# Graph transformer in one launch: the attention's query loads are issued by ScalarE instead of SyncE

## The chip, the cores and the metric

The kernel runs on one core of one Trainium2 chip. The metric is the device time of one execution in microseconds (us). The time before is the median of three runs, 3420.31 us (3411.84 to 3421.84).

## The reference

A graph of 2500 nodes and 40000 edges passes one graph convolution and then a two-layer graph transformer. The attention is over the edges; the kernel computes it densely, with a mask made of edge counts. What matters here is one attention layer:

```python
q = ((x @ Wq[l].T + bq[l]) * scaling).reshape(n, H, DH)      # n = 2500, H = 8, DH = 64
k = (x @ Wk[l].T).reshape(n, H, DH)
v = (x @ Wv[l].T).reshape(n, H, DH)
scores = jnp.einsum('ehd,ehd->eh', q[tgt], k[srcidx])
m = jax.ops.segment_max(scores, tgt, num_segments=n)
p = jnp.exp(scores - m[tgt])
s = jax.ops.segment_sum(p, tgt, num_segments=n)
w = p / (s[tgt] + 1e-16)
agg = jax.ops.segment_sum(w[:, :, None] * v[srcidx], tgt, num_segments=n)
attn = agg.reshape(n, D) @ Wo[l].T + bo[l]
```

## The kernel before

The program has a front (edge counts, graph convolution, first projections), then for each of two layers an attention and a feed-forward part, with projections between the layers, and a final norm. The change is in `attention`, which runs once per layer.

The targets are cut into 20 tiles of 125 nodes, and a tile has 8 heads. A tile and a head make a **unit**, so a layer has 160 units, numbered `u`; `u % 8` is the head, and this text calls the unit with `u % 8 == 0` the tile's unit 0. The 2500 sources are cut into five **chunks** of 500, `k` or `c` from 0 to 4. Each engine has its own program, written out unit by unit and chunk by chunk, and semaphores alone tie them together:

- TensorE scores a chunk against the tile's queries (`score`, L1393), two units ahead of the rest.
- VectorE adds the mask and takes the running maximum (`add_bias`, L1546), then the row's maximum (`maximum`, L1552). At the end of a tile's unit 0 it also scales the sums of the tile before (`normalise`, L1571 to L1578).
- ScalarE takes the exponentials of the next unit in three pieces (`exps`, L1483, which waits for the maximum with `maxed`).
- The weights must be transposed before they multiply the values. Chunks 1 and 3 are transposed by TensorE (`turn_weights`, L1404; then ScalarE's high half L1493 and VectorE's low half L1559). Chunks 0, 2 and 4 are split into two halves in f16 in one of three `staged` buffers (high half by GpSimd for chunks 0 and 2 and by ScalarE for chunk 4, both L1317; low half by GpSimd, L1323), and a DMA transposes the buffer into one of four `across` buffers. That DMA is issued by SyncE (`turn`, L1347). A `staged` buffer is free again when its transposing DMA has landed (`crossed`).
- TensorE multiplies by the values, three chunks later in its own order (`weigh`, L1424).

SyncE issues every transfer of the attention, in one order on one DMA queue: the three transposing DMAs of each unit, one chunk of the next tile's mask before units 1 to 5 (`load_mask`, L1338, two DMAs for 112 and 13 rows), once a layer the output weights (L1364), and the next tile's queries before the transposing DMAs of unit 0 (`load_queries`, L1332, two DMAs of 64 rows with 4000 bytes each, one to each half of the partitions). The queries have two buffers. So their load waits for the maxima of the tile that used the buffer last:

```python
if h == 0:
    if t > 1:
        sp.wait_ge(maxed, U0 + H * (t - 1))
    load_queries(t)
```

Of the kernel before, what the change touches and what calls it, by code (L numbers as in the profile page):

```python
# [30 lines left out]
H = 8  # L31
DH = D // H
# [6 lines left out]
NT = N // P  # L39
# [66 lines left out]
def apart(engine, waits_met):  # L106

    engine.sem_inc(waits_met, 1)
# [1107 lines left out]
def attention(nc, sem, psum, sb, g, layer):  # L1217

    xt, keys, values, vec, q_tiles = g["xt"], g["keys"], g["values"], g["vec"], g["q_tiles"]
    bias_rows, identity, stats = g["bias_rows"], g["identity"], g["stats"]  # L1220
    U0, T0 = UNITS * layer, NT * layer
    EXPS = ((0, 2), (2, 4), (4, 5))
    with ExitStack() as ctx:
        wo_sb = sb(ctx, "wo_sb", [128, FC, D])
        queries = [sb(ctx, f"queries{b}", [128, H, 2, P], F16) for b in range(2)]
# [24 lines left out]
        q_loaded = [sem("q_loaded0"), sem("q_loaded1")]  # L1250
# [3 lines left out]
        maxed = sem("maxed")  # L1254
# [22 lines left out]
        def pe_chunk(u, k):  # L1277
            return len(BY_PE) * (U0 + u) + BY_PE.index(k)

        def dma_chunk(u, k):  # L1280
            return len(BY_DMA) * (U0 + u) + BY_DMA.index(k)

        def dma_chunk_at(n):
            return n // len(BY_DMA), BY_DMA[n % len(BY_DMA)]
# [14 lines left out]
        def use(what, where, part):  # L1299
            n = len(USERS) * layer + USERS.index((what, where, part))  # L1300
            return n, n % TB
# [18 lines left out]
        def low_to_stage(engine, u, k):  # L1320
# [3 lines left out]
                                 prob[u % PROBS][:, k * KC:(k + 1) * KC].rearrange("p (s c) -> p s c", s=BPC),  # L1324
                                 here[0:P, 0:BPC, 0:P], ALU.subtract).then_inc(low_staged[k], 1)

        with nc.Block() as block:
            @block.sync
            def _(sp):
                def load_queries(t):  # L1330
                    for half in range(2):
                        sp.dma_start(queries[t % 2][64 * half:64 * half + 64, :, :, :].rearrange("d h s n -> d (h s n)"),  # L1332
                                     q_tiles[t * DH:(t + 1) * DH, :]).then_inc(q_loaded[t % 2], 16)

                def load_mask(t, c):
                    at = slice(c * KC, (c + 1) * KC)
                    for p0, p1 in CUTS:
                        sp.dma_start(bias[t % 2][p0:p1, at], bias_rows[P * t + p0:P * t + p1, at]).then_inc(mask_loaded[t % 2], 16)  # L1338

                def turn(u, k):  # L1340
                    n = dma_chunk(u, k)
                    if n >= ACROSS:
                        before, chunk = dma_chunk_at(n - ACROSS)
                        sp.wait_ge(weighted, NKC * before + chunk + 1)
                    sp.wait_ge(low_staged[k], U0 + u + 1)
                    apart(sp, g["waits_met"])
                    sp.dma_start_transpose(across[n % ACROSS][:, :, :], staged[n % STAGES][:, :, :].rearrange("p s c -> p (s c)")  # L1347
                                           ).then_inc(crossed[n % ACROSS], 16)

                load_queries(0)  # L1350
                for c in range(NKC):
                    load_mask(0, c)
                for u in range(UNITS):
                    t, h = u // H + 1, u % H
                    if t < NT:

                        if h == 0:
                            if t > 1:
                                sp.wait_ge(maxed, U0 + H * (t - 1))
                            load_queries(t)  # L1360
                        if 0 < h <= NKC:
                            load_mask(t, h - 1)
                        if t == 1 and h == NKC + 1:
                            sp.dma_start(wo_sb[:, :, :].rearrange("p c d -> p (c d)"), g["wo"][layer * 128:(layer + 1) * 128, :]  # L1364
                                         ).then_inc(wo_loaded, 16)
                    for k in BY_DMA:
                        turn(u, k)
# [108 lines left out]
            @block.scalar  # L1476
            def _(act):
                def exps(u, piece):
                    if piece == 0:
                        act.wait_ge(maxed, U0 + u + 1)  # L1480
                    c0, c1 = EXPS[piece]
                    here = prob[u % PROBS][:, c0 * KC:c1 * KC]
                    act.activation(here, here, ACT.Exp, bias=neg_max[u % 4][:, :],  # L1483
                                   accum_out=sums[u // H % 2][:, u % H, piece:piece + 1]).then_inc(exped, 1)

                def high_half(u, k):
                    n, r = use("P", u, k)
                    m = pe_chunk(u, k)
                    act.wait_ge(turned, n + 1)
                    if m >= PB:  # L1490
                        unit, at = divmod(m - PB, len(BY_PE))
                        act.wait_ge(weighted, NKC * unit + BY_PE[at] + 1)
                    act.copy(p_hi[m % PB][:, :], t_ps[r][0:P, 0:KC]).then_inc(p_high, 1)  # L1493

                def read_high(u):
                    act.wait_ge(weighted, NKC * (U0 + u + 1))
                    reached(act, agg_out, U0 + u - 1)
                    act.copy(by_high[u % 2][:, :], o_ps[u % 2][:, 0:DH]).then_inc(high_out, 1)

                def turned_sums(t, half):  # L1500
                    n, r = use("T", t, half)
                    act.wait_ge(turned, n + 1)
                    act.copy(agg_t[t % 2][:, half * 2 * P:(half + 1) * 2 * P], t_ps[r][:, 0:2 * P]).then_inc(agg_turned, 1)  # L1503

                def stage_highs(u, step):

                    for k in BY_DMA:
                        if HIGH_BY[k] == "ACT" and step == min(k // 2 * 2 + 1, NKC - 1):
                            high_to_stage(act, act.copy, u, k)

                for piece in range(len(EXPS)):
                    exps(0, piece)
                for step in range(NKC):
                    stage_highs(0, step)
                for u in range(UNITS):
                    for k in range(NKC):
                        if k in BY_PE:
                            high_half(u, k)
                        if k == LAG and u > 0:
                            read_high(u - 1)  # L1520
                        if k % 2 == 0 and u + 1 < UNITS:
                            exps(u + 1, k // 2)
                        if u + 1 < UNITS:
                            stage_highs(u + 1, k)
                        step = extra_before(u, k)
                        if step and step[0] == "T" and u > H:
                            turned_sums(u // H - 1, step[1])
                read_high(UNITS - 1)
                for half in range(2):
                    turned_sums(NT - 1, half)  # L1530
# [404 lines left out]
```

## Time and profile before

| | |
|---|---|
| median of three runs | 3420.31 us |
| the profiled execution's own time | 3432.88 us |
| its span, first to last instruction | 3431.1 us |
| TensorE's mean granted clock | 0.971 |
| TensorE matmul busy | 3127.8 us (91%) |
| VectorE busy | 2318.9 us (68%) |
| GpSimd busy | 2158.9 us (63%) |
| ScalarE busy | 1954.3 us (57%) |
| DMA queue q1 (SyncE's) | 439.75 MB |
| DMA queue q10 (ScalarE's) | 31.19 MB |

The profile is of one execution, which took 12.57 us longer than the median of the runs; every duration below is from it. The two attention layers are the stretches from about 984 to 1975 us and from 2300 to 3287 us of the span. Times within a view are microseconds from the start of the span, and square brackets in a view hold the time that the engine stood idle ahead of the instruction, and what ended that.

### The profile page before, as it was taken

The numbers are of one execution on the slowest core, as the hardware profiler recorded it, in microseconds if no ns is written. First come the engines' busy times: TensorE is split into PE (matmuls) and PEld (weight loads), VectorE is DVE, ScalarE is ACT, GpSimd is POOL, SyncE is SP. The second block draws the span as 40 slices with busy tenths as digits, with TensorE's granted clock in tenths as the row PEclk, the third lists the DMA queues.
The fourth block names the chain that finished last, engine by engine and source line by source line (L and its number), as shares of the span: only waits on it lengthen the run. The fifth ranks groups of instructions, "written<-read, shape, count | busy, mean of one in ns | idle before, by whom it ended". The sixth has DMA issues, their size and how long they took to land. (4 is left out here: it accounts for less than half of the span.)

```text
span 3431.1 us, 72840 instructions
## 1 busy us (share of the span) xinstructions
PE 3127.8 (91%) x25127; PEld 2478.9 (72%) x25127; DVE 2318.9 (68%) x6932; ACT 1954.3 (57%) x3918; POOL 2158.9 (63%) x1981
## 2 busy tenths in 40 slices
PE   6477999999869999999999989989999999999985
PEld 6343665566548888888888876757888888888874
DVE  7996443443247888888788752237788888888856
ACT  0122444444347777877777711237777777777724
POOL 3788888885047777777777700026777777777734
PEclk9998999999989999999999989999999999999987
DMA  9315667765589999999999811249999999989851
GB/s 341 32 2 104 120 121 124 133 116 113 156 179 167 162 159 169 172 162 164 163 164 163 143 50 37 51 96 170 165 163 164 165 170 167 169 160 169 151 116 60
DMA packets 1290929, 476.32 MB, mean 139 GB/s; under 512 B 1236080, under 2 KB 1261330, under 8 KB 1284873
## 3 DMA queue, kind: packets, MB, share of 16 engines
q1 hardware_dynamic: 1152130, 439.75, 66.9%
q0 software_dynamic: 133120, 0.80, 4.2%
q10 hardware_dynamic: 5320, 31.19, 2.6%
q8 instruction: 199, 3.26, 0.4%
q14 instruction: 160, 1.31, 0.1%
HBM read 133.23 MB, written 80.32 MB: 62 GB/s over the span
## 5 line engine op out<-in xcount | busy, mean ns | idle before, releaser
L1546 DVE CUSTOM_DVE_ANT_0 prob<-s_ps,mask 125x500 f32<-125x500 f32 x1600 | 1058.2, 673 | 307.1 <-PE s_ps L1393 230.5
L1323 POOL TENSOR_TENSOR staged<-prob,staged 125x500 f16<-125x500 f32 x960 | 1067.2, 1117 | 169.1 <-ACT staged L1317 106.6
L1483 ACT ACTIVATE prob<-prob,neg_max 125x1000 f32<-125x1000 f32 (+1 forms) x960 | 954.5, 994 | 123.7 <-DVE scrap L1552 122.6
L1393 PE MATMUL s_ps<-keys,queries 128*125 128x500 f16 x3200 | 946.9, 378 | 39.5 <-DMA queries<-q_tiles 27.0
L529 POOL DMA_INDIRECT counts<-count,cell x320 | 652.8, 2040 | 165.1 <-issue 100.8
L1424 PEld LDWEIGHTS o_ps<-values,across 125*125 125x125 f16 x7680 | 593.3, 139 | 221.8 <-issue 71.1
L1424 PE MATMUL o_ps<-values,across 125*125 125x128 f16 x7680 | 609.4, 223 | 57.2 <-DMA across<-staged 56.2
L1317 POOL CAST staged<-prob 125x500 f16<-125x500 f32 x640 | 385.4, 602 | 390.1 <-ACT prob L1483 248.4
L1559 DVE TENSOR_TENSOR p_lo<-t_ps,p_hi 125x500 f16<-125x500 f32 x640 | 431.9, 675 | 94.9 <-ACT p_hi L1493 94.5
L1404 PE MATMUL t_ps<-identity,prob 125*125 125x125 f32 x2560 | 413.2, 284 | 8.4 <-ACT agg L1503 8.2
L1493 ACT CAST p_hi<-t_ps 125x500 f16<-125x500 f32 x640 | 361.9, 565 | 93.1 <-PE t_ps L1404 92.7
L1393 PEld LDWEIGHTS s_ps<-keys,queries 128*125 128x125 f16 x3200 | 354.9, 139 | 52.7 <-DMA queries<-q_tiles 28.7
L1424 PE MATMUL o_ps<-values,p_hi 125*125 125x128 f16 x2560 | 365.8, 222 | 1.7 <-DVE p_lo L1559 1.7
L1424 PE MATMUL o_ps<-values,p_lo 125*125 125x128 f16 x2560 | 364.6, 222 | 0.0
L1424 PEld LDWEIGHTS o_ps<-values,p_hi 125*125 125x125 f16 x2560 | 323.2, 138 | 52.2 <-DVE p_lo L1559 2.8
L1424 PEld LDWEIGHTS o_ps<-values,p_lo 125*125 125x125 f16 x2560 | 312.2, 139 | 47.3 <-issue 0.6
L1317 ACT CAST staged<-prob 125x500 f16<-125x500 f32 x320 | 195.6, 611 | 259.4 <-issue 204.9
L1404 PEld LDWEIGHTS t_ps<-identity,prob 125*125 125x125 f32 x2560 | 331.7, 189 | 13.2 <-ACT prob L1483 11.0
L1372 POOL MEMSET staged<- 128x1024 f16 x6 | 5.5, 951 | 446.9 <-POOLq L1123 312.1
L1483 ACT ACTIVATION_READ_ACCUMULATOR prob<-prob,neg_max 125x1 f32 x960 | 185.5, 193 | 0.0
L1446 PE MATMUL t_ps<-agg,wo_sb 128*128 128x125 f32 x1280 | 181.1, 287 | 1.1 <-ACT agg L1503 1.1
L969 PE MATMUL agg_ps<-values,turned 125*125 125x512 f32 x400 | 181.2, 592 | 0.0
(170 smaller groups left out, 3900.6 us busy)
## 6 DMA issues: line engine op xcount, KB each, us to landing
mask<-bias_rows SPq DMA_DIRECT2D x200, 218.8 KB
counts<-xt ACTq DMA_DIRECT2D x8, 3054.0 KB, 34.5
keys<-counts SPq DMA_DIRECT2D x40, 546.9 KB
bias_rows<-edge_bias SPq DMA_DIRECT2D x20, 1093.8 KB
queries<-q_tiles SPq DMA_DIRECT2D x80, 250.0 KB, 4.5
across<-staged SPq DMA_TRANSPOSE x960, 3.3
q_tiles<-q_both SPq DMA_DIRECT2D x80, 125.0 KB, 3.0
counts<-count,cell POOLq DMA_INDIRECT x320
```

Of the source, the lines that this page charges most:

```text
L529: pool.indirect_dma_start(counts, bass.IndirectOffsetOnAxis(cell[:, c:c + 1], 0), count[:, c:c + 1], None, compute_op=ALU.add).then_inc(gr ...
L969: mm = pe.matmul(agg_ps[t % 2][0:P, :], lhsT=turned_sb[u % 2][0:P, j * P:(j + 1) * P], rhs=hw(s), start=(s == 0), stop=(s == NT - 1))
L1317: copy(staged[n % STAGES][0:P, 0:BPC, 0:P], prob[u % PROBS][:, k * KC:(k + 1) * KC].rearrange("p (s c) -> p s c", s=BPC)).then_inc(high_st ...
L1323: engine.tensor_tensor(here[0:P, BPC:2 * BPC, 0:P], prob[u % PROBS][:, k * KC:(k + 1) * KC].rearrange("p (s c) -> p s c", s=BPC), here[0:P ...
L1393: mm = pe.matmul(s_ps[n % SB][:, 0:KC], lhsT=queries[b][:, h, part, :], rhs=keys[:, h, c * KC:(c + 1) * KC], start=(part == 0), stop=(part ...
L1404: mm = pe.transpose(t_ps[r][0:P, s * P:(s + 1) * P], prob[u % PROBS][:, (k * BPC + s) * P:(k * BPC + s + 1) * P], identity[0:P, 0:P])
L1424: mm = pe.matmul(o_ps[u % 2][:, 0:2 * DH], lhsT=weights[:, s * step:s * step + P], rhs=values[:, u % H, k * BPC + s, :], start=(k == 0 and ...
L1446: mm = pe.matmul(t_ps[r][:, 0:P], lhsT=wo_sb[:, k, o * 128:(o + 1) * 128], rhs=agg_t[t % 2][:, k * P:(k + 1) * P], start=(k == 0), stop=(k ...
L1483: act.activation(here, here, ACT.Exp, bias=neg_max[u % 4][:, :], accum_out=sums[u // H % 2][:, u % H, piece:piece + 1]).then_inc(exped, 1)
L1493: act.copy(p_hi[m % PB][:, :], t_ps[r][0:P, 0:KC]).then_inc(p_high, 1)
L1546: dve.tensor_tensor_reduce(out=prob[u % PROBS][:, at], in0=s_ps[n % SB][:, 0:KC], in1=bias[b][:, at], scale=1.0, scalar=MASKED, op0=ALU.ad ...
L1559: dve.tensor_tensor(p_lo[m % PB][:, :], t_ps[r][0:P, 0:KC], p_hi[m % PB][:, :], ALU.subtract).then_inc(bank_read, 1)
```

## The change

`load_queries` takes the issuing engine as an argument. ScalarE issues the first tile's queries at the start of the attention, ahead of its first exponential. It issues the queries of tile `t` in unit 0 of tile `t - 1`, right behind the first piece of the next unit's exponentials, and ahead of that it waits for the maxima of the tile before. SyncE keeps its own wait for these maxima, since the mask's buffer needs it too, and keeps the masks, the output weights and all transposing DMAs.

```diff
+        def load_queries(engine, t):
+            for half in range(2):
+                engine.dma_start(queries[t % 2][64 * half:64 * half + 64, :, :, :].rearrange("d h s n -> d (h s n)"),
+                                 q_tiles[t * DH:(t + 1) * DH, :]).then_inc(q_loaded[t % 2], 16)
+
         with nc.Block() as block:
             @block.sync
             def _(sp):
-                def load_queries(t):
-                    for half in range(2):
-                        sp.dma_start(queries[t % 2][64 * half:64 * half + 64, :, :, :].rearrange("d h s n -> d (h s n)"),
-                                     q_tiles[t * DH:(t + 1) * DH, :]).then_inc(q_loaded[t % 2], 16)
-
...
-                load_queries(0)
                 for c in range(NKC):
                     load_mask(0, c)
                 for u in range(UNITS):
                     t, h = u // H + 1, u % H
                     if t < NT:
 
-                        if h == 0:
-                            if t > 1:
-                                sp.wait_ge(maxed, U0 + H * (t - 1))
-                            load_queries(t)
+                        if h == 0 and t > 1:
+                            sp.wait_ge(maxed, U0 + H * (t - 1))
                         if 0 < h <= NKC:
                             load_mask(t, h - 1)
...
+                load_queries(act, 0)
                 for piece in range(len(EXPS)):
                     exps(0, piece)
...
                         if k % 2 == 0 and u + 1 < UNITS:
                             exps(u + 1, k // 2)
+                        if k == 0 and u % H == 0 and u // H + 1 < NT:
+
+                            if u > 0:
+                                act.wait_ge(maxed, U0 + u)
+                            load_queries(act, u // H + 1)
                         if u + 1 < UNITS:
                             stage_highs(u + 1, k)
```

SyncE, around the second tile's unit 0, before the change. `across_0` and `staged_0` stand for all buffers of these names.

```order
452 L1347 DMA_TRANSPOSE across_0<-staged_0 128x8x128 [waits weighted,low_staged4]
453 L1332 DMA queries_0<-q_tiles 64x2000 [waits maxed]
454 L1332 DMA queries_0<-q_tiles 64x2000
455 L1347 DMA_TRANSPOSE across_0<-staged_0 128x8x128 [waits weighted,low_staged0]
456 L1347 DMA_TRANSPOSE across_0<-staged_0 128x8x128 [waits weighted,low_staged2]
457 L1347 DMA_TRANSPOSE across_0<-staged_0 128x8x128 [waits weighted,low_staged4]
458 L1338 DMA mask_0<-bias_rows 112x500
459 L1338 DMA mask_0<-bias_rows 13x500
```

The same place on SyncE with the change.

```order
450 L1347 DMA_TRANSPOSE across_0<-staged_0 128x8x128 [waits weighted,low_staged4]
451 L1347 DMA_TRANSPOSE across_0<-staged_0 128x8x128 [waits low_staged0,maxed,weighted]
452 L1347 DMA_TRANSPOSE across_0<-staged_0 128x8x128 [waits weighted,low_staged2]
453 L1347 DMA_TRANSPOSE across_0<-staged_0 128x8x128 [waits weighted,low_staged4]
454 L1338 DMA mask_0<-bias_rows 112x500
455 L1338 DMA mask_0<-bias_rows 13x500
```

The two query loads ahead of the three transposing DMAs of unit 0 are gone from SyncE, and the wait on `maxed` moved to the first of these three.

ScalarE in the same unit, before the change.

```order
454 L1317 CAST staged_0<-prob_0 125x4x125 [waits stages_cleared,crossed3,exped]
455 L1483 ACTIVATE prob_0,sums_0<-prob_0,neg_max_0 125x1000 [waits maxed]
456 L1493 CAST p_hi_0<-t_ps_0 125x500 [waits weighted,turned]
457 L1483 ACTIVATE prob_0,sums_0<-prob_0,neg_max_0 125x1000
458 L1493 CAST p_hi_0<-t_ps_0 125x500 [waits weighted,turned]
```

ScalarE there with the change (the lines of `attention` behind the moved function are three lower).

```order
456 L1317 CAST staged_0<-prob_0 125x4x125 [waits stages_cleared,crossed3,exped]
457 L1480 ACTIVATE prob_0,sums_0<-prob_0,neg_max_0 125x1000 [waits maxed]
458 L1329 DMA queries_0<-q_tiles 64x2000 [waits maxed]
459 L1329 DMA queries_0<-q_tiles 64x2000
460 L1490 CAST p_hi_0<-t_ps_0 125x500 [waits weighted,turned]
461 L1480 ACTIVATE prob_0,sums_0<-prob_0,neg_max_0 125x1000
462 L1490 CAST p_hi_0<-t_ps_0 125x500 [waits weighted,turned]
```

The two query loads now stand between the next unit's first exponential and the high half of this unit's chunk 1.

## Rows read from the trace of the kernel before

**Rows 1.** Windows view: us, PE, PEld, DVE, ACT, POOL busy, PEclk, DMA share, GB/s

```profile
984.00:1975.00 991.00, 953.68 (x9924) 819.86 (x9925) 799.45 (x2558) 757.62 (x1627) 715.63 (x795) 0.99 0.94 163
```

**Rows 2.** Waits of TensorE in the first layer (total us, times, longest)

```profile
PE o_ps L1424 <- DMA across<-staged: 31.0, 31, 3.7
...
PE s_ps L1393 <- DVE chunk_max L1546: 3.2, 6, 0.6
```

**Rows 3.** Waits of TensorE in the second layer

```profile
PE o_ps L1424 <- DMA across<-staged: 25.3, 29, 3.3
```

**Rows 4.** Timeline of TensorE: chunk 0 of unit 0 in four tiles; chunk 4 in one

```profile
1087.58 0.59 PE L1424 MATMUL o_ps<-values,across 125*125 125x128 f16 x7 [1.51 <-DMA across<-staged]
...
1187.56 0.65 PE L1424 MATMUL o_ps<-values,across 125*125 125x128 f16 x8 [0.89 <-DMA across<-staged]
...
1191.62 0.63 PE L1424 MATMUL o_ps<-values,across 125*125 125x128 f16 x8
...
1928.32 0.63 PE L1424 MATMUL o_ps<-values,across 125*125 125x128 f16 x8
...
3190.70 0.47 PE L1424 MATMUL o_ps<-values,across 125*125 125x128 f16 x5 [0.30 <-DMA across<-staged]
```

**Rows 5.** Timeline of SyncE around unit 0 of the fifth tile

```profile
1180.30 1.23 SPq L1332 DMA_DIRECT2D queries<-q_tiles  x2
1181.65 5.84 SPq L1347 DMA_TRANSPOSE across<-staged  x3
1187.55 1.02 SPq L1338 DMA_DIRECT2D mask<-bias_rows  x2
```

**Rows 6.** Tile view: transposing DMAs issued at 1181.65, 1183.02 and 1924.63

```profile
DMA to landing us min/median/max: 5.8/5.8/5.8
...
DMA to landing us min/median/max: 5.2/5.2/5.2
...
DMA to landing us min/median/max: 3.0/3.0/3.0
```

**Rows 7.** Tile view of all transposing DMAs, then of all query loads

```profile
L1347 SPq DMA_TRANSPOSE across<-staged x960: 1230/1237/4584, 981.0 to 3281.5; - x192
...
DMA to landing us min/median/max: 3.0/3.3/7.5
...
DMA to landing us min/median/max: 3.5/4.5/5.7
```

**Rows 8.** Timeline of GpSimd in that unit

```profile
1180.09 1.10 POOL L1323 TENSOR_TENSOR staged<-prob,staged 125x500 f16<-125x500 f32 x1
...
1181.82 2.26 POOL L1323 TENSOR_TENSOR staged<-prob,staged 125x500 f16<-125x500 f32 x2
1187.57 0.60 POOL L1317 CAST staged<-prob 125x500 f16<-125x500 f32 x1 [3.49 <-issue]
```

**Rows 9.** Timeline of ScalarE in that unit

```profile
1183.55 1.13 ACT L1483 ACTIVATE prob<-prob,neg_max 125x1000 f32<-125x1000 f32 x1 [0.66 <-DVE scrap L1552]
...
1184.67 0.55 ACT L1493 CAST p_hi<-t_ps 125x500 f16<-125x500 f32 x1
...
1189.47 0.61 ACT L1317 CAST staged<-prob 125x500 f16<-125x500 f32 x1 [1.81 <-issue]
```

**Rows 10.** Timeline of VectorE in that unit

```profile
1188.82 0.68 DVE L1546 CUSTOM_DVE_ANT_0 prob<-s_ps,mask 125x500 f32<-125x500 f32 x1 [0.69 <-PE s_ps L1393]
```

**Rows 11.** SyncE, then VectorE, at the start of the second layer's attention

```profile
2280.85 1.13 SPq L1332 DMA_DIRECT2D queries<-q_tiles  x2
2282.03 4.35 SPq L1338 DMA_DIRECT2D mask<-bias_rows  x10
...
2290.55 0.68 DVE L1546 CUSTOM_DVE_ANT_0 prob<-s_ps,mask 125x500 f32<-125x500 f32 x1 [9.98 <-DMA mask<-bias_rows]
```

**Rows 12.** Tile view of ScalarE's own loads of x: issued at 67.2, then 82.6

```profile
L119 ACTq DMA_DIRECT2D x_sb<-x x1: 802/802/802, 67.2 to 67.2; - x1
...
L119 ACTq DMA_DIRECT2D x_sb<-x x1: 505/505/505, 82.6 to 82.6; - x1
```

## The prediction

> **What bounds the kernel now.** I read four views, in this order. The windows view of the first attention layer [rows 1]: TensorE's matmuls are busy 953.68 of 991 us at a clock of 0.99 (the level of 2.4 GHz, nearly throughout), and the next engine, VectorE, 799.45. So TensorE's own stream sets the time of both layers, and every microsecond that it waits there is one of the result. The page's share of busy time doesn't say what it waits for; the view of waits does. In the first layer it waits 31.0 us, in 31 waits, for the DMA that transposes staged weights, and only 3.2 us for VectorE [rows 2]; in the second layer 25.3 us in 29 waits for the same DMA [rows 3]. Together 56.3 us, 1.6% of the span, hang on `across`.
>
> Next I went through TensorE's timeline and noted which unit each of these 60 waits is in. 28 of them, with 24.6 us, are at one place: chunk 0 of a tile's unit 0. The reader sees the first of the 28 (1.51 us), one in the middle (0.89) and the last (0.30) [rows 4]. This is the unit in which SyncE issues the next tile's queries, and there are 36 such loads behind the first tiles (18 a layer). Ten more waits, 13 us, lie in the layers' first tiles, and most of the rest in units 1, 2 and 7.
>
> SyncE's timeline shows why [rows 5]. It issues the queries at 1180.30 (1.23 us for both DMAs), then the three transposing DMAs of the unit from 1181.65. The first lands after 5.8 us and the second after 5.2 us [rows 6], where the median of all 960 is 3.3 and the least 3.0 [rows 7]. The query DMAs take 4.5 us to land (median), so the second, issued some 0.6 us before the transpose, lands just ahead of it. The control is in the same trace: the last tile has no query load in its unit 0. There the first transposing DMA lands after 3.0 us [rows 6], and TensorE's weighing at 1928.32 shows no wait [rows 4].
>
> **The change, part by part.** *SyncE loses the query loads in unit 0.* In the tile of the rows GpSimd's low half of chunk 0 is done at 1180.09 + 1.10 = 1181.19 [rows 8], but SyncE issues at 1181.65, since it is still at the queries. Now it can issue at 1181.3 and the DMA has nothing ahead of it: 3.0 to 3.3 us, so it lands by 1184.6. TensorE was ready at 1187.56 - 0.89 = 1186.67 [rows 4], so 2.1 us are to spare, more than the wait of nearly every other tile. I take the whole of the 28 waits: **-24.6 us**. The bounds are 0 (the wait only moves) and 24.6.
>
> *GpSimd gets its buffers earlier.* It idles 3.49 us until 1187.57, when the first transposing DMA has landed [rows 8], so it is late for units 1 and 2 as well. These two units hold 12.5 us of TensorE's other waits for `across`, some of them due to the mask loads that stay. I take a quarter: **-3 us**, bounds 0 and -12.
>
> *Start of each layer.* SyncE issues queries for 1.13 us ahead of the masks (2280.85 to 2282.03), and VectorE starts at 2290.55, when the last mask has landed, after 9.98 us of idling [rows 11]. The masks now go out 1.2 us earlier, and ScalarE has nothing to do until VectorE has its maxima. Twice 1.2: **-2.4 us**, bounds 0 (the queries' bytes are moved beside the masks' all the same) and -2.4.
>
> *ScalarE gains two issues a tile, right behind the first exponential.* SyncE needs 1.23 us for the pair [rows 5]; the nearest rows of ScalarE's own queue are 0.51 and 0.80 us for one load [rows 12]. I take 1.2. From the exponential's start to the next instruction's are 1184.67 - 1183.55 = 1.12 us [rows 9]. The next cast starts before 1.13 + 0.19 us of the two before it have run one after the other, so instructions are handed over ahead of time, and the issue lies beside the exponential: 0.1 us are left over. Behind it are the high half of chunk 1, VectorE's low half, and VectorE's masking, on which TensorE's scores wait. VectorE idles 0.69 us in that unit [rows 10], which covers it. **0 us.** What if there were no cover: the loads could each have to stand behind a transposing DMA that SyncE is issuing, 1.24 us each [rows 7], so the bounds are 0 and 0.1 + 2 x 1.24 = 2.6 us a tile. The wait on `maxed` added ahead of them is for a maximum two units back, which the exponential in front of it has already outwaited.
>
> *The queries' bytes meet other transposes.* In the tile of the rows ScalarE would issue at 1183.6 to 1184.9, and the data move until about 1188. The low half of chunk 4 is done at 1181.82 + 2.26 = 1184.08 [rows 8], so its transposing DMA now goes out at 1184.2 and shares the DMA engines with the queries. At the worst it takes the 5.8 us of the one behind the queries now [rows 6] and lands at 1190.0. Who waits? TensorE weighs chunk 4 at 1191.62 [rows 4], and without the 0.89 us at 1190.7: not late, by 0.7 us. ScalarE's cast for the next unit, which needs that staged buffer, starts at 1189.47 after 1.81 us of idling [rows 9] and would be 0.5 us later. On average I charge **+3 us** (0.08 a tile); bounds 0 and 24.6 (it costs as much as now).
>
> Sum: -24.6 - 3 - 2.4 + 0 + 3 = -27 us. Against the profiled execution's own time that is 3432.9 - 27 = 3405.9; that one is 12.6 us over the median of the runs, so for the median 3420.3 - 27 = **3393 us**.
>
> One rule speaks against this. The first row above shows two transposes 1.9 to 2.5 us over the median while two query loads of 64 rows with 4000 bytes are ahead of them, and the DMA share of the layer is 0.94 [rows 1], so what is moved matters as well as on which queue. The Trainium skill (DMA: Bandwidth & Descriptors, section "Issuing engines are not separate DMA queues") says that DMAs from different engines run on the same 16 DMA engines and interleave, and that issuing from several saves only issue time. By that rule alone the gain would be SyncE's issue time in 36 tiles and the start, a few microseconds. The trace doesn't contradict it, but shows that what matters is which transpose is in flight: chunk 0 of unit 0 has no slack, chunk 4 has.
>
> **The rivals.** *The wait only moves* (the rule above, as a mechanism here). The queries then delay chunk 4 of unit 0 or chunk 0 of unit 1, and the loop through the staged buffers (ScalarE's cast, GpSimd's low half, SyncE, landing) is as late as now. For it: the bytes are the same, and the DMA share of the layer is already 0.94. Against it: the last tile's control, and 0.7 us of slack behind even the worst landing. It leaves SyncE's 0.46 us in the 28 tiles that wait (13 us at most, some 5 of it likely) and part of the start: 3413 us, 3408 to 3425.
>
> *ScalarE becomes late (ends slower).* If the DMA issues of ScalarE wait while SyncE's transposing DMAs are being issued (three a unit of 1.24 us each, so SyncE issues some 60% of the time), ScalarE's pair takes up to 3.7 us, 2.6 of it uncovered. For it: ScalarE's load took 0.80 us while SyncE was issuing and 0.51 later [rows 12]. Against it: SyncE has 1.2 us less to issue in this very unit, and 0.8 may have been the queue. With VectorE's slack of 0.69 us less the 0.2 it loses with TensorE's wait, a delay `d` costs 36 x (d - 0.5). The gain of 27 us is used up at d = 1.25 us. At d = 1.8 the sum is -27 + 47 = +20: 3440 us; at 2.6 +49: 3469. The Trainium skill (Perfetto Trace Analysis, section "DMA Instruction — HWDGE (DVE, Sync)") says that the descriptor generator is locked for one sequencer at a time and that the lock wait is part of the profiled issue. No row here has ScalarE issuing beside a transposing DMA, so nothing in this trace shows the price.
>
> **How the numbers follow.** The gain as summed 0.61, between 3378 and 3407; the wait only moves 0.22; ScalarE late 0.14; other 0.03. A difference under 0.3% (10 us) can't be told from none in this kernel. Faster: all of the first and a little of the second, 0.62. Within 0.3%: 0.22. Slower: 0.16. The range goes from 3376 (the first case with half of GpSimd's 12 us) to 3432 (the moved wait with some delay of ScalarE); above it lie most of the slow cases, about 0.12.
>
> **What would show it.** Right: the transposing DMAs of chunk 0 in unit 0 land after 3.0 to 3.5 us; TensorE's waits for `across` fall from 56.3 to about 30 us; GpSimd's idling at that place falls from 3.5 to under 1.5 us; the last transposes of unit 0 land later than now without a TensorE wait; VectorE's first masking comes 1.2 us earlier in each layer. Wrong: waits of TensorE on `across` at chunk 2 or 4 of unit 0, or in unit 1, as long as those removed (the wait moved); or ScalarE's pair of issues over 2 us, the high half of chunk 1 late, and TensorE waiting for VectorE well over 3.2 us in the first layer [rows 2] (ScalarE late). Also wrong if the second layer's start doesn't move at all.

## The result: 37 us slower, and the profile after

The changed kernel takes 3456.36 us (median of 4 runs, 3453.79 to 3462.36), the kernel before, run beside it, 3419.39 (4 runs, 3411.84 to 3421.84). The ratio is 1.0106, with a 95% interval of 1.0089 to 1.0123. I had forecast 3393 us, and the time is outside my range too. One execution of all that are reported below, one of the four with the masks on ScalarE's queue, took 10343 us and is left out of that kernel's numbers.

The profiled execution of the changed kernel took 3455.26 us by its own time (before: 3432.88), a span of 3453.4 us. The first attention layer takes 998.7 us from its first weighing on (before 991.5), the second 1004.5 (before 986.8): together 24.9 us more, and everything else 2.5 us less. So the two traces show 22.4 of the 37 us; the kernel before was 12.57 us over its median when it was profiled. Windows view, columns as in [rows 1]: the two layers with the change, then the second layer before it:

```profile
981.40:1980.10 998.70, 956.00 (x9928) 818.57 (x9928) 791.27 (x2553) 755.69 (x1622) 715.67 (x795) 1.00 0.92 162
2304.20:3308.70 1004.50, 960.13 (x9928) 823.58 (x9928) 789.61 (x2553) 756.92 (x1622) 714.21 (x795) 0.99 0.93 161
...
2300.70:3287.60 986.90, 952.64 (x9928) 817.66 (x9928) 797.25 (x2558) 756.84 (x1627) 715.62 (x795) 1.00 0.93 164
```

In the first layer TensorE is busy about as long as before (956.00 us, 954.37 in the same stretch before), in 7 us more. In the second it is also busy 7.5 us longer with the same matmuls. Four times, at 2410.3, 2516.1, 2567.3 and 2669.7, the granted clock is at the lower level (1.2 GHz) for 3.4 us, at the end of a wait of 3.77, 2.85, 2.86 and 3.35 us or right behind it; at half speed that is up to 4 x 1.7 = 6.8 us, an estimate from these rows. The kernel before has no such stretch in this layer behind the first tile. One of the four, the wait and then the windows view:

```profile
2567.05 0.90 PE L1421 MATMUL o_ps<-values,across 125*125 125x128 f16 x8 [2.86 <-DMA across<-staged]
...
2567.30:2570.80 3.50, 3.50 (x24) 2.94 (x23) 0.88 (x3) 3.10 (x5) 3.34 (x5) 0.51 0.70 147
```

TensorE's waits in the first layer, then in the second, which answer to [rows 2, 3]:

```profile
PE o_ps L1421 <- DMA across<-staged: 36.9, 37, 4.0
...
PE s_ps L1390 <- DVE chunk_max L1549: 0.5, 1, 0.5
...
PE o_ps L1421 <- DMA across<-staged: 40.1, 31, 3.8
```

Waits for transposed weights rose from 56.3 to 77.0 us, where I had expected some 30. All transposing DMAs, then all query loads (tile view, [rows 7] before):

```profile
L1347 SPq DMA_TRANSPOSE across<-staged x960: 1231/1235/4416, 975.5 to 3302.2; - x192
...
DMA to landing us min/median/max: 3.0/3.3/8.8
...
L1329 ACTq DMA_DIRECT2D queries<-q_tiles x80: 452/557/1853, 959.5 to 3207.3; - x80
...
DMA to landing us min/median/max: 3.3/4.7/8.9
```

The medians hardly moved; the longest landing went from 7.5 to 8.8 us, and that of the queries from 5.7 to 8.9. One tile shows where (the fourth of the second layer, unit 0). The timelines of SyncE, ScalarE, TensorE and GpSimd:

```profile
2458.02 1.06 SPq L1338 DMA_DIRECT2D mask<-bias_rows  x2
2459.21 7.87 SPq L1347 DMA_TRANSPOSE across<-staged  x3
...
2454.87 1.13 ACT L1480 ACTIVATE prob<-prob,neg_max 125x1000 f32<-125x1000 f32 x1 [0.47 <-DVE scrap L1555]
2454.88 2.36 ACTq L1329 DMA_DIRECT2D queries<-q_tiles  x2
...
2457.34 0.57 ACT L1490 CAST p_hi<-t_ps 125x500 f16<-125x500 f32 x1 [1.24 <-PE o_ps L1421]
...
2463.97 0.61 ACT L1317 CAST staged<-prob 125x500 f16<-125x500 f32 x1 [3.66 <-issue]
...
2457.82 0.63 PE L1421 MATMUL o_ps<-values,across 125*125 125x128 f16 x8
...
2461.85 0.68 PE L1421 MATMUL o_ps<-values,across 125*125 125x128 f16 x8 [1.94 <-DMA across<-staged]
...
2461.95 0.98 POOL L1317 CAST staged<-prob 125x500 f16<-125x500 f32 x1 [4.01 <-issue]
```

Tile view of the transposing DMAs of this unit: the one of chunk 0 (issued 2452.93), of chunk 2 (2454.56), and of chunk 4 (2455.91):

```profile
DMA to landing us min/median/max: 3.0/3.0/3.0
...
DMA to landing us min/median/max: 7.2/7.2/7.2
...
DMA to landing us min/median/max: 8.0/8.0/8.0
```

Chunk 0 lands after 3.0 us, and TensorE doesn't wait for it (2457.82), as I had said. But chunk 2 was issued at 2454.56, **ahead of** the queries (2454.88), if only by 0.32 us, and still lands only after 7.2 us; TensorE waits 1.94 us for it. GpSimd's cast for the next unit waits 4.01 us, until chunk 2 has landed and freed its buffer (2461.8), ScalarE's waits 3.66 us for that of chunk 4, which takes 8.0 us (2463.9), and SyncE, behind them, needs 7.87 us for three transposing DMAs.

The same over all 36 tiles that load, mean landing in us, worked out from the trace (issue to landing, sorted by unit and chunk); the third kernel is the first experiment below:

| transposing DMA | before | with the change | same place, SyncE's queue |
|---|---|---|---|
| unit 0, chunk 0 | 5.0 | 3.7 | 3.7 |
| unit 0, chunk 2 | 4.5 | 5.6 (longest 8.6) | 3.5 |
| unit 0, chunk 4 | 3.4 | 5.2 (longest 8.8) | 4.3 |
| unit 1, chunk 0 | 3.2 | 4.3 (longest 7.1) | 3.8 |

Added up, the four take 16.1 us before, 18.8 with the change, and 15.3 with the load at the same place on SyncE's queue.

How far ahead a transposing DMA is issued matters. Worked out from the same trace: chunk 0 goes out 1.2 to 3.6 us ahead of ScalarE's first query DMA and lands after 3.7 us. Chunk 2 is within 0.8 us of it in 33 of the 36 tiles: in 22 it goes out ahead (mean landing 5.9 us, longest 8.4), in 11 behind (5.8, longest 8.6). In the 3 tiles in which it goes out more than 0.8 us ahead it lands after 3.3 to 3.6 us. SyncE's issue itself takes 1.23 us or more, so the 22 were still being issued when the queries came.

The ledger of TensorE by units, from the start of one unit's first weighing to the next one's, means by layer without the first tile: the interval that ends with the wait of before (unit 7, in the 18 tiles a layer that have a next one) went from 6.25 and 6.24 us to 5.48 and 5.56, 26.4 us saved in all. Unit 0 went from 5.78 and 5.74 to 6.75 and 7.40 us, 49.8 us lost. Unit 1 lost 4.9 us. The first tiles, unit 2 and the layers' last units gave back some 3. (Unit 0 grew by more than the waits within it; in the second layer the lower clock is a part of that.)

### The profile page after: what moved, and what is told of

Read it like the earlier page. It is cut to its first block and busy times, and to the rows that moved or that the text cites. A ratio compares the mean times of both kernels' runs of the same rounds, so it can differ in the third digit from the quotient of the medians.

```text
span 3453.4 us, 72876 instructions
## 1 busy us (share of the span) xinstructions
PE 3130.1 (91%) x25127; PEld 2478.5 (72%) x25127; DVE 2306.5 (67%) x6932; ACT 1955.1 (57%) x3918; POOL 2158.4 (62%) x1981
## 3 DMA queue, kind: packets, MB, share of 16 engines
q10 hardware_dynamic: 11720, 51.67, 5.3%
## 5 line engine op out<-in xcount | busy, mean ns | idle before, releaser
L1421 PE MATMUL o_ps<-values,across 125*125 125x128 f16 x7680 | 611.9, 223 | 77.7 <-DMA across<-staged 77.1
```

Source lines behind the costliest of these rows:

```text
L1421: mm = pe.matmul(o_ps[u % 2][:, 0:2 * DH], lhsT=weights[:, s * step:s * step + P], rhs=values[:, u % H, k * BPC + s, :], start=(k == 0 and ...
```

## The experiments

Three theories could explain it. **Theory 1**: bytes on a second queue delay the transposing DMAs that are in flight, those issued ahead too, where on one queue they delay only what stands behind. **Theory 2**: it is the place; a load between chunks 2 and 4 of unit 0 hits where there is less slack than I thought, whichever engine issues it. **Theory 3**: ScalarE's issues make ScalarE late. All ratios are to the kernel before, run on the same chip; each had the full computation except where stated.

**The change's place on SyncE's queue.**

```diff
-                        if h == 0:
-                            if t > 1:
-                                sp.wait_ge(maxed, U0 + H * (t - 1))
+                        if h == 0 and t > 1:
+                            sp.wait_ge(maxed, U0 + H * (t - 1))
+                        if h == 0 and t == 1:
                             load_queries(t)
...
                     for k in BY_DMA:
                         turn(u, k)
+                        if k == 2 and h == 0 and 1 < t < NT:
+                            load_queries(t)
```

> SyncE issues the query loads again, on its own queue, but at the point of the program where ScalarE's loads fell: between the transposing DMAs of chunk 2 and chunk 4 of unit 0 (the first two tiles' loads stay where they were before). Theory 1 (two queues): what hurts is that query packets on a second queue get in between the packets of transposing DMAs that are already issued; in one queue those are ahead and untouched. Then chunks 0 and 2 of unit 0 land after 3.1 to 3.4 us, chunk 4 after about 5.5, TensorE's waits for across fall below 45 us, and the kernel is 0 to 25 us faster than before (3395 to 3420). Theory 2 (the place): the same bytes a third of a unit later hit more sensitive transposes on whichever queue; then chunk 4 and chunk 0 of unit 1 are late, and the kernel is 15 to 40 us slower than before. Theory 3 (ScalarE is late by its issues): no slowdown here.

3422.52 us, ratio 1.0011 [0.9999, 1.0024]: as before, and 34 us under the change. SyncE's timeline in the fifth tile, then the landing of chunk 4's transposing DMA, the one behind the queries:

```profile
1176.84 2.94 SPq L1347 DMA_TRANSPOSE across<-staged  x2
1179.84 1.88 SPq L1332 DMA_DIRECT2D queries<-q_tiles  x2
1181.84 1.23 SPq L1347 DMA_TRANSPOSE across<-staged  x1
...
DMA to landing us min/median/max: 4.0/4.0/4.0
```

Behind the same bytes on its own queue this one takes 4.0 us, and the mean of the 36 is 4.3, against 5.2 with the change. Theory 2 falls as it stood: the same load about 1 us later costs next to nothing more than before, and so it is at two other places below. But theory 1's numbers were missed as well: I had expected 0 to 25 us of gain, and waits for `across` under 45 us. They are 52.9 us in 73 waits, so the removed ones came back, each smaller, above all at chunk 0 of unit 1 (31 waits, 14.4 us).

**ScalarE issues earlier, and later.** One kernel issues in the unit ahead, near SyncE's old time; the other in unit 4.

```diff
-                        if k == 0 and u % H == 0 and u // H + 1 < NT:
...
-                            load_queries(act, u // H + 1)
+                        if k == 0 and u == 0:
+                            load_queries(act, 1)
+                        if k == LAG and u % H == H - 1 and u // H + 2 < NT:
+                            act.wait_ge(maxed, U0 + u + 1)
+                            load_queries(act, u // H + 2)
```

```diff
-                        if k == 0 and u % H == 0 and u // H + 1 < NT:
...
+                        if k == 0 and u % H == 4 and u // H + 1 < NT:
...
                             load_queries(act, u // H + 1)
```

> ScalarE issues the loads on its own queue, but two thirds of a unit earlier: behind the read of the high sums in the unit ahead of unit 0, about when SyncE issued them in the kernel before. Theory 1 (two queues): transposes already in flight are slowed as in the change (chunk 4 of the unit ahead, chunks 0 and 2 of unit 0), so it is 15 to 45 us slower than before. Theory 2 (the place): as the kernel before, within 10 us. Theory 3 (ScalarE late): the issues lie in another stretch of ScalarE's program, 0 to 30 us slower with the high half of chunk 1 of the next unit late.

> As the change, with ScalarE's loads moved from the tile's unit 0 to its unit 4, where transposed weights lie ready for 2 to 4 us before TensorE takes them in the trace of before. Theory 1 and theory 2 both expect the waits around unit 0 to go (24.6 us in before) with nothing in their place: 15 to 35 us faster than before. Theory 3 (ScalarE late by its issues): the issue costs ScalarE as much as in unit 0, and the time is within 15 us of the change's.

3476.42 us, ratio 1.0162 [1.0145, 1.0180], and 3449.01 us, ratio 1.0078 [1.0051, 1.0104]. At SyncE's old time the loss is larger still, 55 us by the ratio, where theory 1 had 45 at most. It falls on chunk 0 of unit 0 (mean landing 6.7 us), and TensorE's clock falls to the lower level in 14 stretches of 3.4 or 6.8 us behind the first tiles, so that its matmuls are busy 12.5 us longer in the two layers than with the change. In unit 4 the transposing DMAs of chunks 2 and 4 land after 6.6 and 6.1 us, where they take 4.1 and 3.2 when SyncE issues the load in that unit (the next kernel). There I had expected a gain of 15 to 35 us, by slack that did not cover such landings. Moving the issue doesn't make ScalarE's queue as cheap as SyncE's, but the place sets how much it costs.

**SyncE issues in unit 4.**

```diff
-                        if h == 0:
...
+                        if h == (0 if t == 1 else 4):
                             load_queries(t)
```

> The kernel before, with SyncE's loads of tiles 2 to 19 moved from the tile's unit 0 to its unit 4; everything stays on SyncE's queue. Theory 1 and 2: 20 to 35 us faster than before, since the slack of unit 4 covers transposes that land 1 to 2 us late; the first tile as before. Against the same place on ScalarE's queue it shows what the second queue costs where there is slack: theory 1 expects 5 us or more in its favour (the first tile's waits grew by about 4 us a layer in the change), theory 2 none but the first tile's.

3424.50 us, ratio 1.0018 [1.0007, 1.0029]. Waits of TensorE:

```profile
PE o_ps L1424 <- DMA across<-staged: 44.0, 60, 3.0
...
PE s_ps L1393 <- DVE chunk_max L1546: 22.1, 28, 3.1
```

The wait at chunk 0 of unit 0 is nearly gone here too (4.0 of 24.6 us are left), and nothing is gained, where I had expected 20 to 35 us: the waits for `across` fall by only 12 us (56.3 before), and those for VectorE rise by 9.6 (12.5 before). So even without the second queue my 24.6 us were not to be had by moving the whole load into this unit.

**The issues alone.** SyncE loads as before, and ScalarE issues two loads of 64 rows with 12 bytes a tile into a spare buffer at the change's place.

```diff
+                        if k == 0 and u % H == 0 and u // H + 1 < NT:
+                            t1 = u // H + 1
+                            for half in range(2):
+                                act.dma_start(spare[64 * half:64 * half + 64, 6 * t1:6 * t1 + 6],
+                                              q_tiles[t1 * DH:(t1 + 1) * DH, 6 * half:6 * half + 6]).then_inc(spare_in, 16)
```

> The kernel before, and beside it ScalarE issues two tiny loads (64 rows of 12 bytes into a spare tile) at the point of unit 0 where the change put its query loads. So it has the change's issues and the second queue's use, without its bytes. Theory 1 (query packets of the second queue get in between the transposes' packets): as before, within 8 us. Theory 3 (the issues make ScalarE late, or hold up SyncE's issues at a shared descriptor generator): 20 to 40 us slower than before, with the high half of chunk 1 of unit 0 over 0.5 us late.

3424.32 us, ratio 1.0003 [0.9993, 1.0013]. Two issues a tile and nearly no bytes cost nothing that can be measured, though one of them takes ScalarE as long as before with real loads (median 565 ns, 557 with the change). Theory 3 falls: the bytes cost, not the issues.

**Smaller pieces.** Each head's queries stand 12 bytes apart in SBUF, so a row of 4000 bytes moves as eight pieces of 500; once with the change, once on SyncE's queue.

```diff
-        queries = [sb(ctx, f"queries{b}", [128, H, 2, P], F16) for b in range(2)]
+        rooms = [sb(ctx, f"queries{b}", [128, H, 2 * P + 6], F16) for b in range(2)]
+        queries = [room[:, :, 0:2 * P].rearrange("p h (s n) -> p h s n", s=2) for room in rooms]
...
```

> The change with the query tile's heads 12 bytes apart, so that each row of 4000 bytes is moved in eight pieces of 500. Theory 1a (long packets of the second queue hold up the short ones of the transposes, packet for packet): pieces of an eighth of the length let more transposes' packets through in between, so chunk 2 of unit 0 lands sooner than 5.5 us and the kernel is 10 to 30 us faster than the change (3456). Theory 1b (every switch between a transposing and an ordinary packet costs): more switches, so as slow as the change or 5 to 30 us slower than it.

> The same pieces of 500 bytes on SyncE's queue, in the order of the kernel before: the control for e6. In one queue nothing is between the pieces, so both theories expect the kernel before, within 10 us, a little slower if the pieces move more slowly.

On ScalarE's queue 3455.68 us, ratio 1.0097 [1.0080, 1.0113], the same as with whole rows; on SyncE's 3440.12, ratio 1.0050 [1.0032, 1.0067]. Small pieces cost 18 us on the queue of the transposes, where I had expected less than 10, and nothing more on the other, so the second queue costs 37 us with rows of 4000 bytes and 16 with pieces of 500. Theory 1a had 10 to 30 us of gain over the change and falls: the length of a piece doesn't explain the loss. It changes its size.

**The loads left out.** Tiles 3 to 20 use the queries of the first two tiles, and their loads are left out, so this kernel scores 18 of 20 tiles with the queries of another tile.

```diff
-                            load_queries(t)
+                            if t == 1:
+                                load_queries(t)
...
-                    if h == 0 and c == 0:
-                        pe.wait_ge(q_loaded[b], 32 * ((T0 + u // H) // 2 + 1))
+                    if h == 0 and c == 0 and u < 2 * H:
+                        pe.wait_ge(q_loaded[b], 32 * (layer + 1))
```

> The kernel before without the query loads of tiles 2 to 19: the loads of the first two tiles are used for all (the work on them is the same, the output is not). It bounds what any other place or queue for these loads can bring. If the 24.6 us of waits in unit 0 are the kernel's to gain, it is 25 to 40 us faster than before (3380 to 3395). If they cover other waits, which take their place (VectorE's masks, as e4 shows 16 us more of them), it is 0 to 12 us faster.

3379.58 us, ratio 0.9876 [0.9860, 0.9893]. Windows view of the first layer, which is from about 980 to 1945 us here:

```profile
980.00:1945.00 965.00, 947.02 (x9917) 818.28 (x9915) 794.95 (x2558) 758.34 (x1623) 711.53 (x794) 1.00 0.90 158
```

TensorE's waits:

```profile
PE o_ps L1425 <- DMA across<-staged: 24.9, 28, 2.9
```

The DMA share falls from 0.94 to 0.90 and the time by 43 us. That is the price of the 36 loads before the change, 1.2 us each; 24.6 us of it were visible as waits in unit 0. With the change they cost about 43 + 37 = 80 us, 2.2 each (the 37 include what the loads of the first two tiles cost there). The 16 us in the expectation are all of the waits for VectorE in that kernel's layers; 9.6 us are more than before.

**Half of the bytes.** One of a load's two halves on ScalarE's queue at the change's place, the other on SyncE's ahead of unit 0.

```diff
+                load_queries(sp, 0)
...
+                            load_queries(sp, t, (1,))
...
-                load_queries(act, 0)
...
-                            load_queries(act, u // H + 1)
+                            load_queries(act, u // H + 1, (0,))
```

> One of a load's two halves (64 rows of 4000 bytes, one half of the partitions) is issued by ScalarE at the change's place, the other stays on SyncE ahead of unit 0; the first tile's and second tile's loads: the first on SyncE, the second split as well. What theory 1 expects (bytes of a second queue slow the transposing DMAs in flight, per byte): half of the change's loss, +18 us, about 3437, TensorE's waits for across some 65 us. If instead any use of the second queue beside the transposing DMAs costs it whole, however few the bytes (against the run with 12-byte loads, which had almost none): +35. If halves that spread over time are cheaper: 3420 or less.

3432.36 us, ratio 1.0022 [1.0011, 1.0033], that is 7.5 us by the ratio and 10.6 by the medians: a fifth to over a quarter of the change's loss for half of its bytes, where theory 1 by the byte asked for +18. The loss grows faster than the bytes in one burst.

**Another load on the second queue.** The queries stay on SyncE, and ScalarE issues the masks in units 1 to 5.

```diff
-                        if 0 < h <= NKC:
-                            load_mask(t, h - 1)
...
+                        if k == 0 and 0 < u % H <= NKC and u // H + 1 < NT:
+                            load_mask(act, u // H + 1, u % H - 1)
```

> The queries stay on SyncE as before, and ScalarE issues the next tile's mask instead (a chunk of 125 rows of 2000 bytes in two DMAs in each of units 1 to 5, behind the first piece of the exponentials). Theory 1 (bytes on a second queue beside transposing DMAs cost them more than bytes on their own queue): a tile's mask has 1.25 MB against 0.51 MB of queries, so by bytes 2.4 times the change's loss, +90 us, 3510; if only a burst of 0.5 MB at once hurts and 0.25 MB in each unit find slack, under +20. The theory that it is the place in unit 0, or the layout of the queries, that makes the loss: no change, 3420.

3505.25 us (median of three runs), ratio 1.0248 [1.0226, 1.0271]. The waits of TensorE:

```profile
PE o_ps L1422 <- DMA across<-staged: 128.1, 135, 3.9
```

The page's row of ScalarE's queue (packets, MB, share of 16 engines):

```profile
q10 hardware_dynamic: 34580, 78.71, 8.1%
```

This queue moved 31.19 MB before (the table above), so these are 47.5 MB more for 84 us: 1.8 us per MB. With the change it is 20.5 MB (51.67 less 31.19) for 37 us: 1.8 us per MB too. So it is nothing about the queries, their layout or unit 0: another load in other units is dear as well beside these transposing DMAs once it is on the other queue. Theory 1 had put +90 us on record for it. That the two prices per MB are equal is in part luck, for other kernels here give others: with ScalarE at SyncE's old time 55 to 58 us for 20.5 MB, 2.7 and more; in unit 4 1.0 to 1.2 (20.5 us over SyncE in unit 4 by the ratios, 24.5 by the medians); with pieces of 500 bytes 0.8 (16 us over the same pieces on SyncE's queue); with half of the bytes 0.8 to 1.1.

**Only the first tile's queries on ScalarE.**

```diff
-                load_queries(0)
...
+                load_queries(act, 0)
                 for piece in range(len(EXPS)):
                     exps(0, piece)
```

> Only the first tile's queries of each layer are issued by ScalarE, all others stay on SyncE. My prediction's term for the start was -2.4 us (VectorE's first masking 1.2 us earlier in each layer); the rule that queues only share the DMA engines gives 0. In the trace of the change VectorE's start and TensorE's first weighings tell: if the gaps of chunk 0 of unit 0 of the first tiles stay at the 1.5 and 1.1 us of before, the 4.1 and 3.0 us seen with the change come from the second tile's queries.

3425.37 us, ratio 1.0003 [0.9992, 1.0014]. VectorE at the start of the second layer in this kernel's timeline:

```profile
2281.39 0.68 DVE L1546 CUSTOM_DVE_ANT_0 prob<-s_ps,mask 125x500 f32<-125x500 f32 x1 [9.93 <-DMA mask<-bias_rows]
```

The same instruction in the changed kernel, and TensorE's first weighing of each layer there:

```profile
2292.12 0.68 DVE L1549 CUSTOM_DVE_ANT_0 prob<-s_ps,mask 125x500 f32<-125x500 f32 x1 [9.26 <-DMA mask<-bias_rows]
...
981.38 1.11 PE L1421 MATMUL o_ps<-values,across 125*125 125x128 f16 x8 [4.05 <-DMA across<-staged]
...
2304.23 0.85 PE L1421 MATMUL o_ps<-values,across 125*125 125x128 f16 x8 [2.99 <-DMA across<-staged]
```

VectorE waits 9.93 us against 9.98 [rows 11]: with the same bytes beside them the masks land no earlier, though SyncE no longer issues the queries ahead of them. The first weighings waited 1.48 and 1.14 us before, 1.25 here in the first layer, and 4.05 and 2.99 with the change, so that wait comes from the second tile's queries.

**A version that gains.** All on SyncE's queue, and a load's halves apart: one in unit 7 of the tile ahead, one in unit 0, each between chunks 0 and 2.

```diff
-                            load_queries(t)
+                            if t == 1:
+                                load_queries(t)
...
                     for k in BY_DMA:
+                        if k == 2 and h == H - 1 and 1 < t + 1 < NT:
+                            sp.wait_ge(maxed, U0 + u + 1)
+                            load_queries(t + 1, (0,))
+                        if k == 2 and h == 0 and 1 < t < NT:
+                            load_queries(t, (1,))
                         turn(u, k)
```

> All on SyncE's queue: one half of a load (tiles 3 to 20) goes out in unit 7 of the tile ahead between the transposing DMAs of chunks 0 and 2, the other half in unit 0 at the same place. If the price of a load is its time on the DMA engines ahead of a transposing DMA, two short delays of 0.6 us each hide better than one of 1.2, since each is nearer to the slack: 3405 to 3415. If the total bytes alone count (43 us for all loads): 3419, no change.

3409.03 us, ratio 0.9961 [0.9948, 0.9974]: 13 us faster than the kernel before and 47 us faster than the changed one, and inside what I had expected. TensorE's waits, and then, in the tile view, the landings of all its transposing DMAs:

```profile
PE o_ps L1430 <- DMA across<-staged: 30.6, 40, 2.9
...
PE s_ps L1399 <- DVE chunk_max L1552: 22.0, 28, 3.4
```

```profile
DMA to landing us min/median/max: 3.0/3.3/6.5
```

The waits for `across` fall by 26 us, about what I had promised of the change; 9.5 us of them come back as waits for VectorE. The longest landing is 6.5 us. This kernel changes two things at once, the halves and the place (between chunks 0 and 2), and no run tells which of them gains.

## Why the prediction was wrong

**What bounds the kernel: right.** TensorE's stream sets the time and its waits for `across` are the lever: over the runs, time rises with them, though not one for one (24.9 us of waits at 3379.6, 30.6 at 3409, 52.9 at 3422.5, 77.1 at 3456, 86.8 at 3476, 128.1 at 3505).

**SyncE loses the loads, -24.6: right as a wait, wrong as a gain.** The waits at chunk 0 of unit 0 fell from 24.6 us in 28 to 2.2 in 4, and its landing from 5.0 to 3.7 us. But the run with the loads in unit 4 of SyncE, which removes the same waits, gains nothing. The wait was the first place at which a load's DMA time showed, and not the whole of its price (43 us).

**GpSimd earlier, -3: wrong in sign.** Its buffers come later in the changed kernel (4.01 us of idling in the tile shown, 3.49 in the tile of [rows 8]), and waits for `across` in unit 1 went from 3.8 us to 14.8.

**Start, -2.4: nearly nothing.** VectorE's wait fell by 0.72 us in the second layer's start; with only the first tile's queries moved, by 0.05. My lower bound (the bytes are moved beside the masks all the same) was the truth, and I hadn't counted that the second tile's queries meet the first transposing DMAs (4.05 and 2.99 us of wait). They brought forward waits that the first tiles had anyway: these tiles' waits for `across` are 13.3 us before and 13.7 after.

**ScalarE's issues, 0: right.** Shown by the run with tiny loads. In single tiles the pair takes long (2.36 us above), but ScalarE being late was not the cause, though the measured time lies between the two that this rival gave (3440 and 3469).

**The queries' bytes meet other transposes, +3: this step failed.** I took for the worst landing the 5.8 us of a transpose that stands behind the queries *on one queue*, found 0.7 us of slack behind it for chunk 4, and asked about chunk 4 alone. Measured are up to 8.8 us for chunk 4. Chunk 2 takes up to 8.4 us where it is issued ahead of the queries, and 3.5 (mean) with the same load behind it on one queue. TensorE's waits at chunks 2 and 4 of unit 0 went from none to 33.7 us, and 11.0 were added in unit 1: 44.7 us, where my upper bound was 24.6. The bound was no bound, since it assumed that the price of the bytes doesn't depend on the queue. Both runs on that question (same place on SyncE: 1.0011 [0.9999, 1.0024]; masks on ScalarE: +84 us) say that it does. What I hadn't weighed at all is the clock: in the second layer's trace it fell at four of the long waits, and TensorE's longer busy time is 7.5 of the 17.7 us.

**The range's lower end.** 3376 doesn't follow from the ground that I gave: with 6 us for GpSimd the sum is 3390. Nothing hangs on it, since the time is above the range.

The rival *the wait only moves* had the mechanism, the wait did move to chunk 2 of unit 0 and chunk 0 of unit 1; its price was wrong, as it took the moved wait to be no longer than the old one. The Trainium skill (DMA: Bandwidth & Descriptors, section "Issuing engines are not separate DMA queues") says that it only saves issue time to spread DMAs over engines. The runs agree that nothing is gained, and show that it isn't neutral: 37 us lost. Open too is why half of the bytes bring so little of the loss, and whether a load that goes out on the second queue clear of every transposing DMA is free; the three tiles with 3.3 to 3.6 us hint at it.

## What to carry to other kernels

Where the path hangs on the landing of small latency-bound DMAs, try bulk loads on the same queue, behind them, and in parts that go out in different units (ratio 0.9961 here): a load on another queue is not out of the way, it delayed even those issued up to 0.8 us ahead of it. The wait that a transfer causes is where its DMA time shows first; to know what the transfer costs, leave it out once, and only then ask what moving it can give. A bound taken from rows holds only for the arrangement of these rows: one queue's worst landing says nothing about two queues. And a wait can cost more than its own length, where the clock falls with it.

## What the runs showed of the hardware

The DMA engines' total work did not grow. The page's rows of SyncE's and ScalarE's queue in the changed kernel:

```profile
q1 hardware_dynamic: 1145730, 419.27, 63.8%
q10 hardware_dynamic: 11720, 51.67, 5.3%
```

Together that is 69.1% of a span of 3453.4 us, 2386 us, and before it was 2385 (66.9 + 2.6% of 3431.1 us). So the loss is not more work for the DMA engines: it is the same packets in the same total time, in an order in which what TensorE waits for lands later. TensorE's clock, by the rows above: at four waits of 2.85 to 3.77 us the granted clock was 0.50 to 0.51 for 3.4 us. And two small issues of ScalarE amid transposing DMAs that take SyncE 1.24 us each cost nothing measurable (ratio 1.0003).
